# One order of steps for attention that runs across pairs of batches

## The reference

```python
# x (16, 224, 512), context (16, 750, 384), 8 heads of 64, mask over the keys
q, k, v = ln(x) @ W_q, context @ W_k, context @ W_v
attn = softmax(where(mask, q k^T * scale, -max))
x = x + (attn v) @ W_o + b_o
# experts: top 2 of 8, capacity 1120, relu(xe @ W1[e]) @ W2[e], weighted, added
x = x + experts(ln(x))
```

## Time and profile before

| what | us |
|---|---|
| median of 3 runs (2270.47 to 2272.11) | 2272.09 |
| the profiled execution's own time | 2268.47 |
| its span | 2266.7 |
| unit 0 of the first pair starts at | 48.85 |
| unit 0 of the second pair / of the last pair | 136.90 / 644.30 |
| attention's last matmuls (`lg`) end near | 721.5 |

### The profile page before, as it was taken

The page is one execution under the profiler, slowest core; times in us unless marked ns, Lnnn a source line. Parts: engine busy times, 40 slices in busy tenths (PEclk is TensorE's granted clock), DMA queues, the critical chain, the costliest instruction groups (busy, mean ns, idle before and its releaser), DMA issues.

```text
span 2266.7 us, 30701 instructions
## 1 busy us (share of the span) xinstructions
PE 2097.9 (93%) x12006; PEld 1857.3 (82%) x12006; DVE 994.7 (44%) x2207; ACT 677.9 (30%) x1672; POOL 511.5 (23%) x551
## 2 busy tenths in 40 slices
PE   4898898898896399999999999999999999999997
PEld 3877877877884399899989889998888899988997
DVE  5665666666665633422422342242224345224221
ACT  3533633633542222311321131132113124113110
POOL 1542543543543411110101111010110111110100
PEclk9999999999997599999999999999999999999999
DMA  4122022022012332420421242042124325113211
GB/s 142 48 80 67 13 79 69 11 79 72 7 49 71 120 84 46 133 54 14 119 73 28 46 133 54 14 121 71 28 42 132 60 45 160 27 33 122 41 14 15
DMA packets 95533, 148.40 MB, mean 65 GB/s; under 512 B 7920, under 2 KB 49312, under 8 KB 95376
## 3 DMA queue, kind: packets, MB, share of 16 engines
q1 hardware_dynamic: 79632, 109.36, 15.1%
q0 software_dynamic: 15744, 36.71, 9.2%
HBM read 110.66 MB, written 35.39 MB: 64 GB/s over the span
## 4 chain that ended last, share of the span: by engine, by line
PE 65%; DVE 1%; issue 1%; DMA 0%; POOL 0%; POOLq 0%; ACT 0%; DVEq 0%
PE psH L1410 31%; PE psY L1410 31%; PE psX L1424 1%; PE psI L1455 1%; DMA xg<-xn_rows,gid 0%; DVE onehot L1307 0%; POOL out_dram L1236 0%; POOL xg L1227 0%; DVE moves L1299 0%; POOLq L1157 0%; DVE xg L1349 0%; DVE xg L1369 0%; DVE xg L1352 0%; DVE ys L1364 0%; DVE w_lo L942 0%
## 5 line engine op out<-in xcount | busy, mean ns | idle before, releaser
L1390 DVE SCALAR_TENSOR_TENSOR hT_lo<-psH,hT_hi 128x384 fp32r<-128x384 f32 (+1 forms) x384 | 209.9, 546 | 944.6 <-ACT hT_hi L1266 939.2
L1266 ACT ACTIVATE hT_hi<-psH 128x384 fp32r<-128x384 f32 (+1 forms) x384 | 185.2, 482 | 1124.5 <-PE psH L1410 1119.2
L1410 PE MATMUL psH<-xgT_hi,w_hi 128*128 128x384 f32 (+2 forms) x1536 | 484.8, 316 | 9.5 <-issue 8.8
L1410 PE MATMUL psH<-xgT_lo,w_hi 128*128 128x384 f32 (+2 forms) x1536 | 482.9, 314 | 4.9 <-issue 4.9
L1410 PE MATMUL psH<-xgT_hi,w_lo 128*128 128x384 f32 (+2 forms) x1536 | 484.0, 315 | 0.0
L1410 PE MATMUL psY<-w_hi,hT_hi 128*128 128x512 f32 (+1 forms) x1002 | 402.7, 402 | 0.0
L1410 PE MATMUL psY<-w_hi,hT_lo 128*128 128x512 f32 (+1 forms) x1002 | 394.2, 393 | 0.0
L1410 PE MATMUL psY<-w_lo,hT_hi 128*128 128x512 f32 (+1 forms) x1002 | 394.1, 393 | 0.0
L1410 PEld LDWEIGHTS psH<-xgT_hi,w_hi 128*128 128x128 f32 x1536 | 290.5, 189 | 33.8 <-issue 17.4
L1410 PEld LDWEIGHTS psH<-xgT_lo,w_hi 128*128 128x128 f32 x1536 | 290.6, 189 | 21.0 <-issue 5.7
L1410 PEld LDWEIGHTS psH<-xgT_hi,w_lo 128*128 128x128 f32 x1536 | 290.3, 189 | 0.0
(11 more groups left out here) (187 smaller groups left out, 2965.6 us busy)
## 6 DMA issues: line engine op xcount, KB each, us to landing
stage<-in_L_ffn_W_dram SPq DMA_DIRECT2D x128, 512.0 KB
x_sb<-in_x_dram SPq DMA_DIRECT2D x8, 896.0 KB, 8.1
x_res<-in_x_dram SPq DMA_DIRECT2D x8, 896.0 KB, 5.7
out_dram<-x_res SPq DMA_DIRECT2D x8, 896.0 KB, 4.8
xn_rows<-xn SPq DMA_DIRECT2D x8, 896.0 KB, 4.8
c_sb<-in_ctx_dram SPq DMA_DIRECT2D x16, 375.0 KB
out_dram<-zrow SPq DMA_DIRECT2D x9, 256.0 KB, 4.4
xg<-xn_rows,gid POOLq DMA_INDIRECT x72
```

The costliest lines, as they stand in the source:

```text
L1266: nc.scalar.activation(hT[0][:, f % 2, 0:m], psH[f % 2][:, 0:m], ACT.Relu).then_inc(h_hi, 1)
L1390: nc.vector.scalar_tensor_tensor(out=hT[1][:, f % 2, 0:m], in0=psH[f % 2][:, 0:m], scalar=0.0, in1=f32(hT[0][:, f % 2, 0:m]), op0=ALU.max, ...
L1410: mm = nc.tensor.matmul(out, stationary(a, c), moving(b, c), start=first and c == chunks[0] and j == 0, stop=last and c == chunks[-1] and ...
```

## The change

`steps` no longer ends a pair. Unit 0 of pair p stands right behind unit 15 of pair p-1, and the last `t` and `o` of pair p-1 are in units 0 to 3 of pair p. The table `PLACED` puts the projections behind steps of units: `wo`, `tt` and `lg` of the pair *before* (in units 3 to 13), `v`, `q`, `k` of this pair, and `fx`, `fc`, `q0`, `k0` of the next one (units 10 to 14). VectorE's statistics and scaling of x (`fs`, `fa`, `fp`), the second LayerNorm's scaling (`ap`) and the mask's bias (`mb`) are steps of the list as well. `tt` 0 and 1, which went through `psT`, go through `psJ`. After the last pair a list `LAST_STEPS` finishes its units and its output projection. The weights come in the order `wk`, `wq`, `wv`, `wo`, and those of `wv` and `wo` are split during units of the first pair (`SPLIT_LATER`); ahead of unit 0 stand only `fc`, `fx`, `k0`, `q0`. GpSimd adds the bias to the residual in units 11 to 14. What is computed is the same.

```diff
-FRONT = [("fx", 0), ("fx", 1), ("fx", 2), ("fx", 3), ("fc", 0), ("fc", 1), ("fc", 2)]
-def steps(nxt):
-    out = [("s", 0), ("s", 1), ("v", 2), ("v", 3), ("s", 2)]
-    for u in range(3, NU):
-        if u in (3, 6, 10):
-            hp = {3: 1, 6: 2, 10: 3}[u]
-            out += [("q", hp), ("k", hp)]
-        out.append(("s", u))
-        out.append(("t", u - LT))
-        if u - LT - 1 >= 0:
-            out.append(("o", u - LT - 1))
-        if nxt and u > 10:
-            out.append(FRONT[u - 11])
...
+PLACED = {
+    (0, "o"): [("q", 1)],
+    (1, "o"): [("k", 1), ("fs", 0), ("fs", 1)],
+    (2, "s"): [("v", 0)], (2, "o"): [("v", 1), ("fs", 2), ("fs", 3)],
+    (3, "t"): [("fa", 0)], (3, "o"): [("wo", 0)],
+    (4, "s"): [("wo", 1)], (4, "o"): [("fp", 0), ("v", 2)],
+    (5, "s"): [("v", 3)], (5, "o"): [("wo", 2), ("ap", 0)],
+    (6, "s"): [("fp", 1)], (6, "o"): [("wo", 3), ("ap", 1)],
+    (7, "s"): [("q", 2)], (7, "t"): [("ap", 2)], (7, "o"): [("k", 2)],
+    (8, "s"): [("ap", 3)], (8, "o"): [("q", 3), ("fp", 2)],
+    (9, "o"): [("k", 3), ("fp", 3)],
+    (10, "s"): [("tt", 0)], (10, "t"): [("fx", 0)], (10, "o"): [("tt", 1)],
+    (11, "s"): [("fx", 1)], (11, "t"): [("tt", 2)], (11, "o"): [("fx", 2)],
+    (12, "s"): [("tt", 3)], (12, "t"): [("fx", 3)], (12, "o"): [("fc", 0)],
+    (13, "s"): [("fc", 1)], (13, "t"): [("fc", 2)], (13, "o"): [("lg", 0)],
+    (14, "s"): [("lt", 0), ("q", 0)], (14, "o"): [("k", 0)],
+    (15, "t"): [("mb", 0)],
+}
+SPLIT_LATER = {("s", 0): ("wv", 0), ("s", 1): ("wv", 1), ("k", 1): ("wv", 2),
+               ("s", 4): ("wo", 0), ("s", 5): ("wo", 1), ("s", 6): ("wo", 2), ("s", 7): ("wo", 3)}
...
 def proj(...):
-                if (p is not None or at >= 2) and (kind, i) not in (("tt", 0), ("tt", 1)):
...
+                if p is not None or at >= 2:
+                    pe.wait_ge(proj_done, at - 1)
...
 def iteration(...):        # GpSimd
+                    if u in (11, 12, 13, 14):
+                        t = u - 11
+                        if t == 0:
+                            pool.wait_ge(xr_in, 16 * p + 16)
+                        nc.gpsimd.tensor_tensor(xr[:, t, :], xr[:, t, :], T["bias"][:], ALU.add).then_inc(biased, 1)
```

More of the change, by code:

```diff
@@ L188, in split_steps @@
-def split_steps(nxt):
-    out = steps(nxt)
+PLACED = {
[16 rows of a table added]
+}
+OF_PREVIOUS = ("wo", "ap", "tt", "lg", "lt")
+OF_NEXT = [("fx", 0), ("fx", 1), ("fx", 2), ("fx", 3), ("fc", 0), ("fc", 1), ("fc", 2), ("q", 0), ("k", 0),
+           ("fs", 0), ("fs", 1), ("fs", 2), ("fs", 3), ("fa", 0), ("fp", 0), ("fp", 1), ("fp", 2), ("fp", 3), ("mb", 0)]
+LAST_STEPS = [("t", -3), ("o", -4), ("t", -2), ("o", -3), ("wo", 0), ("t", -1), ("o", -2), ("wo", 1), ("o", -1), ("ap", 0),
+              ("wo", 2), ("ap", 1), ("tt", 0), ("wo", 3), ("ap", 2), ("tt", 1), ("ap", 3), ("tt", 2), ("tt", 3), ("lg", 0), ("lt", 0)]
@@ new lines, in steps @@
+def steps(prev, nxt):
+    if prev and nxt is None:
+        return LAST_STEPS
+    out = []
+    for u in range(NU):
+        for kind, i in (("s", u), ("t", u - LT), ("o", u - LT - 1)):
+            if prev or i >= 0:
+                out.append((kind, i))
+            out += [x for x in PLACED.get((u, kind), []) if (prev or x[0] not in OF_PREVIOUS) and (nxt or x not in OF_NEXT)]
+    return out
+PRO_ORDER = [("fc", 0), ("fc", 1), ("fc", 2), ("fx", 0), ("fx", 1), ("fx", 2), ("fx", 3), ("k", 0), ("q", 0)]
@@ new lines, with ring_order @@
+SPLIT_AT = {("fx", 0): "wk", ("k", 0): "wq"}
+SPLIT_LATER = {("s", 0): ("wv", 0), ("s", 1): ("wv", 1), ("k", 1): ("wv", 2),
+               ("s", 4): ("wo", 0), ("s", 5): ("wo", 1), ("s", 6): ("wo", 2), ("s", 7): ("wo", 3)}
+RINGED = ("q", "k", "v", "fx", "fc", "wo", "tt", "lg")
+SPLIT = ("fx", "fc", "v", "q", "k")
+def ring_order(prev, nxt):
+    return [x for x in steps(prev, nxt) if x[0] in RINGED]
+NPRO, NITER, NFIRST = len(PRO_ORDER), len(ring_order(True, True)), len(ring_order(False, True))
@@ L191, in split_steps, with ring_start, with_order @@
+HITER = sum(k in SPLIT for k, _ in ring_order(True, True))
+assert (NPRO + NFIRST) == NITER and NITER % 2 == 0
+def ring_start(p):
+    if isinstance(p, int) and p == 0:
+        return NPRO
+    if isinstance(p, int) and p == NPAIR:
+        return NITER * (NPAIR - 1) + len(ring_order(True, False))
+    return NITER * p
+def with_order(src_steps):
+    out = list(src_steps)
     for n in range(len(out) - 1):
@@ L252, in m_row, with index, ring, bank @@
             return v[:, b, SK - NKEY:SK].partition_broadcast(R)
[L254 to L267, removed]
+        def index(p, prev, nxt, kind, i):
+            return (PRO_ORDER if p is None else ring_order(prev, nxt)).index((kind, i))
+        def ring(p, prev, nxt, kind, i):
+            return index(p, prev, nxt, kind, i) + (0 if p is None else ring_start(p))
+        def bank(p, prev, nxt, kind, i):
+            first = 0 if p is None or not isinstance(p, int) else ring_start(p)
+            return psJ[(first + index(p, prev, nxt, kind, i)) % 2]
+        def hi_count(p, prev, nxt, kind, i):
             if p is None:
                 return PRO_ORDER.index((kind, i)) + 1
-            return [x for x in order(nxt) if x[0] in SPLIT].index((kind, i)) + 1 + HPRO + HITER * p
+            return [x for x in ring_order(prev, nxt) if x[0] in SPLIT].index((kind, i)) + 1 + NPRO + HITER * p
         def v_half(src, h):
             return src[0:KC, 0:D].rearrange("p (a h d) -> p a h d", h=2, d=DH)[:, :, h, :]
+        def chunk_at(name, n):
+            return PARTS[name][0] + n
+        def unit(i):
+            return (i % NU) // 4, (i // 2) % 2, i % 2
         block = ctx.enter_context(nc.Block())
@@ L282, in load_mask, with load_ahead, rows_out, load_rows @@
                     sp.dma_start(m_sb[:, b, :], m_row(p, b)).then_inc(m_in, 16)
-            def iteration(p, nxt):
-                sp.dma_start(xr[:], rows(A["x"], p)).then_inc(xr_in, 16)
[L287 to L300, removed]
+            def load_ahead(p):
+                sp.wait_ge(proj_mm, ring_start(p) - 2)
+                load_front(sp, T, A, p + 1)
+                sp.wait_ge(mbias, p + 1)
+                load_mask(p + 1)
+            def rows_out(p, prev, nxt):
+                sp.wait_ge(proj_done, ring(p, prev, nxt, "wo", TP - 1) + 1)
+                sp.dma_start(rows(A["out"][0:NTOK, :], p - 1), xr[:]).then_inc(x2_out, 16)
+                sp.wait_ge(xn2_done, TP * p)
+                sp.dma_start(rows(A["xn2"], p - 1), xn2[:]).then_inc(xn2_out, 16)
+                sp.wait_ge(x2_out, 16 * p)
+                held(sp, passed, xn2_out, 16 * p)
+            def load_rows(p):
+                sp.dma_start(xr[:], rows(A["x"], p)).then_inc(xr_in, 16)
             load_mask(0)
@@ L322, in front_ln, with tail_ln, iteration @@
                 rstd(n, var1, mv1[:, :, 1], rs1[:, :], eps1, rs1_done, TP)
[L324 to L327, removed]
+            def tail_ln(p, t):
+                rstd(TP * p - TP + t + 1, var2, mv2[:, t, 1:2], rs2[:, t:t + 1], eps2, rs2_done, 1)
+            def iteration(p, prev, nxt):
                 for u in range(NU):
@@ L602, in proj, with iteration @@
                 mm.then_inc(proj_mm, 1)
-                if kind == "lg":
-                    held(pe, passed, lg_copied, p + 1)
-                    for t in range(TP):
-                        mm = nc.tensor.transpose(out[0:R, TP * R + t * E:TP * R + (t + 1) * E], lgT[:, t * R:(t + 1) * R], ident[0:E, 0:E])
-                    mm.then_inc(lg_t, 1)
-            def iteration(p, nxt):
-                for kind, i in steps(nxt):
-                    hp, b, h = i // 4, (i // 2) % 2, i % 2
+            def iteration(p, prev, nxt):
+                for kind, i in steps(prev, nxt):
+                    hp, b, h = unit(i)
+                    early = not prev and i < 2
                     if kind == "s":
                         if i == 0:
-                            first = isinstance(p, int) and p == 0
-                            pe.wait_ge(proj_done, (ring(None, True, "k", 0) if first else ring(p - 1, True, "k", 0)) + 1)
+                            pe.wait_ge(proj_done, ring_start(p))
                         elif i % 4 == 0:
-                            pe.wait_ge(proj_done, ring(p, nxt, "k", hp) + 1)
-                        if i >= 2:
+                            pe.wait_ge(proj_done, ring(p, prev, nxt, "k", hp) + 1)
+                        if not early:
                             pe.wait_ge(masked, NU * p + i - 1)
```

245 lines of the change are left out of this document (126 added, 119 removed), and 3 rows, old and new, of the table ITER_ORDER.

## The result

The changed kernel takes 2297.92 us in the median (2293.3 to 2302.11, 4 runs) against 2272.1 (2270.47 to 2273.1) for the kernel before, run beside it: a ratio of 1.0122 [1.0099, 1.0144], slower by some 26 us or 1.2%. The forecast was 2298. The profiled execution took 2299.55, its span is 2297.8.

The account below looks back on a forecast made before the run. Bound: the loop of mask, exponentials, hi, lo, next mask through two in-order queues. Middle pairs +7, start -14.1 and end +23.6 (together +16.7), clock +10: +27 on 2268.5 is 2295, plus 3.6 for the median 2298; range 2258 to 2322.

Parts of the forecast that it names:

- (1): Ahead of unit 8 in a middle pair, `k` 2: TensorE waits 2.8 us for late VectorE's `k_lo`.
- (2): `fx` 0 in unit 10: TensorE waits 2.4 us for the last scaling of x, behind `k_lo` 3 on VectorE.
- (3): Units 10 to 13, three small transposes each: waits of 1.1 and 1.6 at `fx` 1 and 2, 1.1 at `fc` 1, 1.8 at `lg`.
- the +7: Six middle pairs without clock loss: 85.8 us each, +1.2 for each, +7 us in all.
- (4): Small waits elsewhere in a middle pair (`o` 15, `tt`, `fx` 3, `fc` 0): 1.3 us.
- The clock: TensorE at half speed after long waits: one drop of 1.65 us charged in each of six pairs, +10 us.
- The start and the end: Pair 1 starts at 122.8 instead of 136.90, -14.1 us; the last pair takes 101.0 instead of 77.4, +23.6.
- The edits at nothing: GpSimd's bias steps in units 11 to 14, 1.3 us each, were costed at nothing.
- VectorE keeps up: Rival: VectorE's lateness from unit 5 to 10 is absent, middle pairs 79 us; -32, 2240 us; chance 0.15.
- Full clock: Rival: the walked waits hold but don't lower the clock; +17, 2289 us; chance 0.20.
- More clock: Rival: clock falls also in units 10 to 13, `lg` at half speed, +2.7 in each of six pairs; 2314 us; chance 0.18.
- No change: Rival: gains at the pair's turn and the start pay for the rest; 2272 us; chance 0.07.

Follow-up runs that it names:

- e5: Changed kernel with ScalarE's exponentials put behind the transposes' steps and `t` in units 6, 8 and 10 to 13: 2270.68 us, 1.0005 of the kernel before.
- e7: Kernel before the change, with ScalarE taking `oT_hi` and the transposed block's hi part ahead of the exponentials in units 11 to 14: 2253.05 us, 0.992.
- e1: Changed kernel with `q` 2 and `k` 2 moved to unit 6, `wo` 3 and `ap` 1 to unit 7: 2274.22 us, 1.0037 of the kernel before.
- e4: Changed kernel with `fp` 3, the last scaling of x, ahead of `k` 3: 2296.43 us, 1.0131 of the kernel before.
- e2: Changed kernel with ten idle 512-column matmuls ahead of unit 8 from the second pair on: 2289.29 us, 1.0103 of the kernel before.
- e6: Changed kernel with e1, e3 and e5 together: 2247.46 us, 0.9898 of the kernel before.
- e3: Changed kernel with the weights of `v` ahead of the first loads of x, context and mask in SyncE's queue: 2289.79 us, 1.0095 of the kernel before.

## Why the prediction was right

**Which work bounds.** Right. The loop of mask, exponentials, hi, lo and next mask through queues in program order was named as the bound, and e5 and e7 show it in both kernels: moving one step in one queue takes out 27 and 17 us with every engine doing the same work.

**(1) The wait at `k` 2.** 2.46 against 2.8, at its place and by its mechanism (VectorE late for `k_lo`, e1). The terms printed, 1.9 + 6.2 - 5.6, make 2.5; the other 0.3 has no row.

**(2) `fx` 0.** 1.75 against 2.4. The chain behind `k_lo` 3 fits (e4); the lateness of VectorE that the walk carried to it is less.

**(3) Units 10 to 13.** 0.84 and 1.31 against 1.1 and 1.6, 0.78 against 1.1, 1.39 against 1.8: all there, each a quarter too long. Together (1) to (3) are 8.6 against 10.8, and the middle pair without clock is 84.59 against 85.8. This is the term that was mis-sized: the +7 was 0, since 84.59 is the old length. Of the 1.3 of (4) no wait is named; in the pair of 87.48, work of 73.9, named waits of 8.6 and a clock loss of 2.9 leave 2.1 us that no row explains.

**The clock.** The sum was right by luck, its parts were not. I charged +10, one drop of 1.65 us in each of six pairs. Measured are +9.3, none in two pairs, 1.6 and 1.9 in two (0.35 of the 1.9 behind `fx` 0), 2.9 in two. That a wait of some 2.5 us where TensorE is the bound costs clock, and that one where VectorE is the bound doesn't, was argued and is now shown (e2, and the windows from `fx` 0 to `fx` 2). The Trainium skill, page "TensorE: Matmul & The Clock Gate", section "HAM oscillation — how this bites in real kernels", has bursts behind long enough waits start at half rate. Its example has waits of 3 to 5 us. The waits here are shorter, and the traces agree for four of the six of 2.46 and four of the six of 1.75, while two of each kept 1.00. I had priced +23 by taking every wait near 2 us as long enough, which that section doesn't say; the profile shows less than half of it, because some waits cost no clock and the drops behind `fx` 0 cost next to nothing. So the middle pairs are +9.4 where +17 was foretold, 7.6 too many.

**The start and the end** took that back. Unit 0 came at 43.74 (44.5), the wait for the weights of `v` was 8.19 (7.4), though SyncE issued the mask in 1.71 us in place of the 6.0 of the earlier trace rows: the weights were issued from 38.48 on instead of 44.5, but ScalarE got them only at 52.57 (51), 14.1 us later where I had taken 6.5. Two errors cancelled there. The first pair is 83.3 against 78.3. Of the missing 5.0 the wait for the weights has 0.8. The other waits named behind unit 0 come to 10.3, where I had charged 17, so what is missing lies elsewhere: it may be half speed, for which I charged nothing (the pair's clock is 0.86), but no run took that apart. So -9.9 stands against -14.1. The last pair is 107.56 against 101.0, and this its windows split:

```profile
643.84:688.90 45.06, 43.03 (x257) 37.11 (x255) 27.32 (x80) 20.58 (x64) 18.50 (x26) 1.00 0.07 21
688.90:698.90 10.00, 10.00 (x56) 9.30 (x56) 4.39 (x13) 3.80 (x11) 1.73 (x2) 0.83 0.46 137
698.90:709.50 10.60, 8.27 (x74) 7.88 (x72) 7.41 (x23) 6.35 (x21) 6.84 (x8) 1.00 0.17 46
709.50:724.36 14.86, 12.82 (x70) 8.08 (x71) 6.95 (x22) 6.04 (x19) 10.00 (x11) 0.89 0.01 2
724.36:751.40 27.04, 20.43 (x92) 12.83 (x92) 11.97 (x24) 0.90 (x2) 3.61 (x8) 0.94 0.21 68
```

The pair's own ending, the last row, is 27.0 against 28.2. Ahead of it are 80.5 against 72.8: the sum charged the last pair no clock, and it loses at most (1 - 0.83) x 10.00 = 1.7 behind unit 8 and (1 - 0.89) x 14.86 = 1.6 in the fourth row. The other 4.4 stay open. The waits named there come to 6.4 against my 6, so they are not the reason; e6, which loses no clock there and waits for only 2.9, still has 73.5 (from 597.66 to 671.20). With +1.4 behind attention, 26.7 - 7.6 + 4.2 + 6.6 + 1.4 is 31.3, and the profiled executions differ by 2299.55 - 2268.47 = 31.1. The changed kernel's median lies 1.6 below its profiled execution, where I had added 3.6 for before's: the sum alone was 4.4 too low (2295.2 against 2299.55), and this hid it. That the forecast met the median to 0.1 us is luck: the terms were 7.6 too much and 12.2 too little, 5.2 went the other way between profiled execution and median, and the printed sum (2268.5 + 26.7 + 3.6) is 2298.8, not 2298.

**The edits at nothing.** GpSimd's bias steps cost nothing that can be seen: with them in place e6's middle pairs go down to 79.0. No run took them out.

**The rivals.** VectorE keeps up (2240): no, all its waits are there. Full clock (2289): no. e2, with nearly no clock cost in the middle pairs, has a median of 2289.3, but that is 23 us above the kernel before beside it, not 17: its first and last pairs are still too long. More clock (2314): no, `lg` still takes 3.17 in middle pairs, and 4.87 and 4.57 in the last one alone. No change: no.

## What to carry to other kernels

When three engines share one list in program order, ask for each queue who needs the next step soonest: results that TensorE wants three units later were ahead of those that it and VectorE waited for, and moving them gave more than a new order of the whole pair. Removing a place where TensorE runs short moves the shortage to where small transposes pile up, unless the engines that empty the banks get room for them. A wait of TensorE of some 2 us is to be priced with the clock behind it where TensorE is the bound, and without it where another engine is; who is the bound can change with the next edit (the drop behind `fx` 0 costs 0 to 0.35 us in the changed kernel and some 0.9 in e6).

## What the runs showed of the hardware

The same wait of 2.46 us, at the same place of a loop, left the granted clock over the next ten microseconds at 1.00, 0.83 or 0.68. The pairs took 84.59, 86.17 to 86.18, 86.44 to 86.49 or 87.48 to 87.51, in both profiles of this kernel, dealt out differently. So the clock's fall doesn't follow from the wait alone; what decides it was not measured.

Filling a wait with matmuls whose result nobody reads shortened the six middle pairs from 516.8 to 507.4 us (e2), by what the clock kept.

How long SyncE was held by one and the same transfer differed. The changed kernel's issues from the mask on:

```profile
35.81 1.71 SPq L322 DMA_DIRECT2D m_sb<-in_mask_BxS_bk_dram  x2
...
38.48 4.30 SPq L348 DMA_DIRECT2D x2T<-in_L_xattn_W_v_dram  x3
```

The mask took 6.01 in the kernel before, 1.71 here and 2.88 in e3. A term priced by one row of issue was 4.3 too long; which of the transfers ahead of it makes the difference was not tried.
